# Keys' norms and factors computed between the query projections, queries' norms between the inverse levels, sums of squares taken as rows

## The reference, cut to what matters

```python
q = _short_conv(hidden_states @ Wq.T, conv_q)   # 4 taps over time, then silu; the same for k and v
beta = sigmoid(hidden_states @ Wb.T)
q = q * rsqrt(sum(q * q, -1) + 1e-06)           # per token and head; the same for k
A = where(tri_strict, -((k * beta) @ k.T), 0)   # in chunks of 32 tokens
T = solve_triangular(eye - A, eye, lower=True)
u = T @ (v * beta);  w = T @ (k * beta)
attn = where(causal, q_i @ k_i.T, 0)
o = p0 * fir3(v) + p1 * fir15(v) + p2 * fir63(v) + p3 * delta_out + p4 * v
```

## Time and profile before

| | |
|---|---|
| median of 3 runs (lowest to highest) | 488.44 us (485.57 to 488.8) |
| the profiled execution: its time / its span | 488.29 us / 486.5 us |
| busy in the span | TensorE 92%, VectorE 65%, ScalarE 34%, GpSimd 16% |
| mean granted TensorE clock | 0.969 of 2.4 GHz |

### The profile page before, as it was taken

The page is one execution under the profiler, slowest core; times in us unless marked ns, Lnnn a source line. Parts: engine busy times, 40 slices in busy tenths (PEclk is TensorE's granted clock), DMA queues, the critical chain, the costliest instruction groups (busy, mean ns, idle before and its releaser), DMA issues.

```text
span 486.5 us, 8118 instructions
## 1 busy us (share of the span) xinstructions
PE 445.5 (92%) x3154; PEld 290.7 (60%) x3154; DVE 317.7 (65%) x596; ACT 164.6 (34%) x208; POOL 78.7 (16%) x77
## 2 busy tenths in 40 slices
PE   1998889899998997899999979999998899999985
PEld 1962334335554574658776537886445688888862
DVE  5441134567993889998647874552214999999955
ACT  2001211255730010113233153204005788788730
POOL 2000000000004590001552110047200000000061
PEclk9998999999998599999978999999999999999998
DMA  8999916934040415006400020037607999999644
GB/s 323 427 427 424 428 58 248 294 76 98 1 172 14 130 49 159 3 1 259 177 3 0 2 86 0 1 120 234 231 1 292 371 398 381 384 420 385 240 113 167
DMA packets 17937, 92.41 MB, mean 190 GB/s; under 512 B 3424, under 2 KB 5104, under 8 KB 10736
## 3 DMA queue, kind: packets, MB, share of 16 engines
q1 hardware_dynamic: 14880, 78.82, 42.9%
q10 hardware_dynamic: 1488, 8.93, 5.3%
q0 software_dynamic: 1536, 4.20, 2.6%
HBM read 82.25 MB, written 12.08 MB: 194 GB/s over the span
## 4 chain that ended last, share of the span: by engine, by line
PE 75%; DVE 18%; issue 3%; ACT 2%; POOL 1%; DMA 1%; SPq 0%; DVEq 0%; ACTq 0%
PE bank L823 32%; PE bank L664 7%; PE bank L599 5%; PE bank L632 5%; PE bank L526 3%; PE bank L496 3%; PE bank L547 3%; PE bank L506 3%; DVE ring L1337 3%; DVE part L1337 3%; PE bank L648 2%; PE bank L800 1%; PE bank L649 1%; POOL small L415 1%; DVE ring L1426 1%
## 5 line engine op out<-in xcount | busy, mean ns | idle before, releaser
L599 PE MATMUL bank<-xnT,ring 128*128 128x512 f32 x96 | 43.2, 599 | 0.7 <-ACT xnT L962 0.7
L1337 DVE SCALAR_TENSOR_TENSOR part<-ring,cols,part 128x504 f32<-128x504 f32 (+13 forms) x64 | 42.6, 728 | 0.1
L664 PEld LDWEIGHTS bank<-ring 64*64 64x64 f32 x960 | 33.3, 140 | 14.2 <-issue 13.2
L664 PE MATMUL bank<-ring 64*64 64x64 f32 (+1 forms) x960 | 37.7, 231 | 2.9 <-issue 2.7
L632 PE MATMUL bank<-early,ring 128*32 128x512 f32 (+15 forms) x512 | 35.2, 422 | 1.4 <-DVE early L1360 1.4
L415 POOL TENSOR_TENSOR small<-small 128x1 f32<-128x1 f32 (+2 forms) x11 | 11.3, 1025 | 154.4 <-DVE small L1224 81.1
L1337 DVE SCALAR_TENSOR_TENSOR ring<-bank,cols,ring 128x504 f32<-128x504 f32 (+2 forms) x36 | 26.4, 734 | 12.6 <-ACT ring L1009 11.6
L599 PEld LDWEIGHTS bank<-xnT,ring 128*128 128x128 f32 x96 | 17.6, 190 | 20.9 <-issue 20.0
L632 PEld LDWEIGHTS bank<-early,ring 128*32 128x32 f32 x512 | 14.4, 114 | 18.2 <-issue 12.9
L1073 ACT ACTIVATE ring<-bank 128x256 f32<-128x256 f32 x20 | 7.7, 384 | 50.3 <-PE bank L664 49.9
L1115 ACT ACTIVATE rows<-bank 128x512 f32<-128x512 f32 x19 | 11.4, 599 | 36.0 <-PE bank L823 36.0
(11 more groups left out here) (245 smaller groups left out, 914.6 us busy)
## 6 DMA issues: line engine op xcount, KB each, us to landing
early<-wffn_in SPq DMA_DIRECT2D x21, 1024.0 KB, 8.1
ring<-ctxT_in SPq DMA_DIRECT2D x4, 2048.0 KB, 27.3
ring<-ctx_in SPq DMA_DIRECT2D x4, 2048.0 KB, 31.7
raw1b<-wffn_in SPq DMA_DIRECT2D x6, 1024.0 KB, 9.7
raw3b<-wffn_in SPq DMA_DIRECT2D x6, 1024.0 KB, 7.6
raw2b<-wffn_in SPq DMA_DIRECT2D x6, 1024.0 KB, 8.5
ring<-firw_in SPq DMA_DIRECT2D x4, 1024.0 KB, 5.2
xs<-zeros_in ACTq DMA_DIRECT2D x1, 3840.0 KB, 13.9
```

The lines of the kernel that those rows point to most:

```text
L599: last = pe.matmul(bank[5 + g % 3][:, :], wqkv[:, j, c, h * P:(h + 1) * P], xnT[:, c, :], start=(c == 0), stop=(c == DC - 1))
L664: last = pe.matmul(dst[s, d], left[s, L * t:L * (t + 1)], right(s, t), start=True, stop=True)
L1337: return dve.scalar_tensor_tensor(out=d, in0=s, scalar=w, in1=d, op0=ALU.mult, op1=ALU.add)
```

## The change

Names as before; lines move by up to 140, so the pieces name functions.

- A head's sum of squares is no longer 4 products with one output column. Squares of four heads are kept, `sum_rows` sums them as four rows of 32 partitions in a bank (4 products of 32x512 side by side), ScalarE copies the bank, and `turn_sums` turns it into 16 columns (4 products of 4 columns). It is done twice, for the keys behind projections 9 and 10, for the queries behind the keys' products. The power on GpSimd is twice 16 columns wide.
- The keys' power, table (4 rows, `ct_k`), factors, scaling and masking come before and around the last projection and its convolution; the queries' (20 rows, `ct_q`), their factors, scaling, scores and masks between the steps of the first pair of levels.
- v is transposed behind projections 8 to 11, and ScalarE scales it by beta in 4 pieces of 128 columns a head (VectorE did it whole). Tap 0 of the two short filters goes to ScalarE too (`tap0_done`).
- The long filter of head 0 begins behind projection 9, head 1's stretches into the levels, heads 2 and 3 take 4 rounds a step. The weights have three places in place of two and are loaded from projection 4 on, each as its part of the projections' weights is done with.
- Twelve 20-column gate instructions become three of 80; twelve for the table become three. Both `keep_warm` calls of the stage go. Projections use banks 1, 5, 6.

```diff
+                    sp.wait_ge(S["qkv_done"], H * (h + 1))
+                else:
+                    sp.wait_ge(S["fir_done"], 1)
+                i = h % 3
+                sp.dma_start(flat[:, FIRN * i:FIRN * (i + 1)], firw_in[h]).then_inc(ld_firw[h], 16)
 
             build_stack(0)
...
+            load_firw(2)
             build_stack(2)
-            load_firw(2)
+            load_firw(3)
             build_stack(3)
-            load_firw(3)
             sp.wait_ge(S["fir_done"], H)
-            sp.wait_ge(S["sumsq_done"], 2 * H)
+            sp.wait_ge(S["sumsq_done"], 2)
 
...
-            def sumsq(i):
-                pe.wait_ge(S["sq_done"], i + 1)
+            def sum_rows(k):
+
+                pe.wait_ge(S["sq_done"], H * (k + 1))
+                for i in range(H):
+                    last = pe.matmul(bank[4][CG * i:CG * (i + 1), :], ones[:, 0:1].broadcast_to([P, CG]), sq_b[:, i, :],
+                                     start=True, stop=True)
+                last.then_inc(S["cols_done"], 1)
+
+            def turn_sums(k):
+
+                pe.wait_ge(S["cols_kept"], 2 * k + 1)
                 for t in range(NT):
-                    last = pe.matmul(bank[4][:, 256 + NT * i + t:257 + NT * i + t], sq_b[:, i % 2, t * P:(t + 1) * P],
-                                     ones[:, 0:1], start=True, stop=True)
+                    last = pe.matmul(bank[4][:, 16 * k + t:16 * (k + 1):NT], sum_row[:, t * P:(t + 1) * P],
+                                     ident[:, 0:P:CG], start=True, stop=True)
                 last.then_inc(S["sumsq_done"], 1)
+
+            def fir_rounds(h, lo, hi):
+
...
-            for h in range(H):
-                pe.wait_ge(S["silu_done"], h + 1)
-                if h == 2:
-                    keep_warm(bank[2][:, :], 4)
+                if 2 * H - 1 <= g < 3 * H - 1:
+                    turn_v(g - 2 * H + 1)
+                if g == 2 * H:
+                    fir_rounds(0, 0, 4)
+                    sum_rows(0)
+                if g == 2 * H + 1:
+                    turn_sums(0)
+                if g == 2 * H + 2:
+                    fir_rounds(0, 4, 8)
+                    turn_table(1, 3, 20, 24)
+
...
+                    spread(bank[4 + k % 2][:, :], ct_q, (k // 4) * NPROB + (0, 1, 2, 4)[k % 4]).then_inc(S["bc_done"], 1)
 
             def between_first(step):
 
-                fir_rounds(2 + step // NLV, FW * (step % NLV) // NLV, FW * (step % NLV + 1) // NLV)
+                if step == 0:
+                    fir_rounds(1, 10, 13)
+                if step == 1:
+                    fir_rounds(1, 13, FW)
+                    turn_table(2, 4, 0, H * NPROB)
+                if 2 <= step < 6:
+                    fir_rounds(2, 4 * (step - 2), 4 * (step - 1))
+                if step >= 6:
+                    fir_rounds(3, 4 * (step - 6), 4 * (step - 5))
+                if step in (3, 4):
+                    pe.wait_ge(S["ct_lo"], 2)
+                    query_factor(2 * step - 6)
+                    query_factor(2 * step - 5)
+                if step == 6:
+                    query_scores(0)
+                    query_scores(1)
+                if step == 7:
+                    query_scores(2)
+                if step == 8:
+                    query_scores(3)
...
                 if j > 0:
-                    i = g - H
-                    act.wait_ge(S["silu_done"], g + 1)
-                    if i >= 2:
-                        act.wait_ge(S["sumsq_done"], i - 1)
-                    act.activation(sq_b[:, i % 2, :], plane[j][:, h], ACT.Square).then_inc(S["sq_done"], 1)
-
+                    act.activation(sq_b[:, h, :], plane[j][:, h], ACT.Square).then_inc(S["sq_done"], 1)
+                else:
+                    for medium, last_tap in ((0, KS - 1), (1, KS + KM - 1)):
+                        w = C_FIR + h * (KS + KM) + last_tap
+                        act.activation(branch[medium][:, h], vP[:, h], ACT.Copy,
+                                       scale=cols[:, w:w + 1]).then_inc(S["tap0_done"], 1)
+
+                act.wait_ge(S["cols_done"], 2 * k + 2)
+                act.activation(table[:, 0, :], bank[b][0:table.shape[0], :], ACT.Copy).then_inc(S["cols_kept"], 1)
+
+            def scale_values(h):
+
+                act.wait_ge(S["vt_done"], h + 1)
+                for t in range(NT):
+                    ts = slice(t * P, (t + 1) * P)
+                    ins = act.activation(bv[:, h, ts], bank[2 * (h % 2)][:, ts], ACT.Copy, scale=beta[:, t, h:h + 1])
...
             lag0(0)
             for g in range(1, 3 * H):
+                if g == 2 * H + 1:
+                    keep_sums(0)
+                if g == 3 * H - 1:
+                    keep_table(0, ct_k, 3)
                 lag0(g)
...
                     gate_exp(g - H - 1)
+                if g >= 2 * H:
...
+
+            convolve(0)
+            for g in range(1, H):
+                convolve(g)
+                fir_taps(g - 1, g)
+            convolve(H)
+            fir_taps(3, 6)
+            convolve(H + 1)
+            gating_1()
+            clear_heads(0)
+            fir_taps(6, 7)
+            convolve(H + 2)
+            gating_2()
+            convolve(H + 3)
+            clear_heads(1)
+            fir_taps(7, 8)
+            convolve(2 * H)
+            gating_3()
+            fir_taps(8, 12)
+            want_powers(0)
+            convolve(2 * H + 1)
+            key_table()
+            fir_taps(12, 13)
+            convolve(2 * H + 2)
+            fir_taps(13, 17)
+            table_low(0, ct_k, 3)
+            for h in range(H):
+                scale_key(h)
+            convolve(3 * H - 1)
+            mask_keys(0)
+            mask_keys(1)
+            want_powers(1)
+            mask_keys(2)
+            mask_keys(3)
...
+
             for n in range(2 * NLV):
-                if n in (0, NLV - 1):
-                    clear_heads(2 + (n > 0))
-                fir_taps(first + taps * n // (2 * NLV), first + taps * (n + 1) // (2 * NLV))
+                if n == 1:
+                    query_table()
+                if n in (2, 5):
+                    clear_heads(2 + n // 5)
+                if n == 3:
+                    table_low(1, ct_q, 4)
+                if n in (4, 5):
+                    scale_query(2 * n - 8)
+                    scale_query(2 * n - 7)
+                if n == 7:
+                    mask_scores(0)
+                    mask_scores(1)
+                if n == 8:
+                    mask_scores(2)
+                if n == 9:
+                    mask_scores(3)
```

269 lines of the change are left out of this document (135 added, 134 removed).

## The result

| | before | after |
|---|---|---|
| median (lowest to highest) | 488.38 us (485.08 to 489.65), 10 runs | 490.42 us (489.91 to 491.26), 10 runs |
| ratio after/before, 95% interval | | 1.0061 (1.0035 to 1.0087) |
| profiled execution: time / span | 488.29 / 486.5 us | 490.5 / 488.7 us |
| mean granted clock | 0.969 | 0.962 |
| first projection to the experts' first product | 202.0 us | 205.0 us |

The change costs about 2 us. 485.8 had been forecast, a gain of 2.5. The last row of the table is the stretch with all that the change touches, and what follows it on unchanged code. It starts with the first projection (89.69 before, 88.68 after) and ends with the first product of the shared experts (291.72 and 293.70). What is left of the span behind it is 194.8 and 195.0 us. So it is the stretch by which the kernels are compared here.

The account below looks back on a forecast made before the run. It took the stretch from 89 to 225 as bound by a row of waits and slow products. About 9 us saved at full clock less 6.5 for half clock gave 488.3 - 2.5 = 485.8 us, range 478.5 to 491.

Parts of the forecast that it names:

- TensorE up to the last projection: TensorE's work through the last projection, sums out, filter rounds and v in: end moves from 137.5 to 144.7.
- The wait that is added: Behind the last projection the first key factor waits for ScalarE's scaled v: TensorE stands 3.3 us, until 148.0.
- The clock: TensorE behind the added wait: half clock from 148 to 164.5, 6.5 us lost.
- GpSimd's power of 16 columns: The power on GpSimd, now 16 columns wide: 2.9 us, where 32 columns took 5.44.
- The levels: First pair of levels, VectorE setting the pace: 46.4 us from 168.4 to 214.8 at full clock, against 224.9 before.
- The sum: Whole kernel: about 9 us saved at full clock, 6.5 lost to half clock, so 2.5 saved.
- the slower rival: Half clock in TensorE's pauses inside the levels makes VectorE wait, about 10 us more: 495.8 us, chance 0.14.
- Its lesser form: Within the levels, only one group of products ahead of VectorE's masks runs at half clock: 490 us.
- The first rival: The clock stays full behind the last projection despite the added wait: 479.3 us, chance 0.28.
- Its signs of being wrong: ScalarE's pieces 0.6 each, added wait under 1.5, filter weights after 127, or clock dips elsewhere; expected no VectorE level wait over 3.

Follow-up runs that it names:

- e2: Changed kernel with four unread products filling TensorE's pause behind the last projection, the wait itself kept: 487.65 us, ratio 0.9957.
- e3: Changed kernel with GpSimd's ten mask products of the second pair held until 8 updates of the first: 488.88 us, ratio 0.9987.
- e4: Changed kernel with VectorE making the first update and the query table ahead of seven filter taps: 489.26 us, ratio 0.999.
- e6: Changed kernel with GpSimd's ten mask products of the second pair started after 7 updates, where VectorE waits for scores: ratio 0.9941.
- e11: Changed kernel with the edits of e1 and e7, and GpSimd's second-pair products split, two after 7 updates, eight after the first pair: 474.72 us, ratio 0.9728.
- e7: Changed kernel with TensorE making query factors and scores ahead of the four filter rounds of the same step: ratio 0.9994.
- e12: e11 plus the edit of e4 (first update and query table ahead of seven taps): 475.83 us, ratio 0.9715.
- e1: Changed kernel with ScalarE scaling the last head of v ahead of tap 0 of the last projection: 483.72 us, ratio 0.9868.

## Why the prediction was wrong, by its own steps

- **TensorE up to the last projection**: right in its end, 144.4 against 144.7, with some luck. The wait for the filter's weights is 2.2 in place of 0.5, near the upper bound of 2.6 given; the stage began 1.0 earlier, and the other terms came out 1.0 smaller.
- **The wait that is added**: right. 3.03 us against 3.3, four pieces in 1.12 against 1.2.
- **The clock**: the fall was forecast rightly, the return wasn't. Half clock from 147.6 to 157.8, not 148 to 164.5. The forecast let it return 3.5 us into head 1's round 0; that round began at 159.5, when the clock was full already. e2 puts the price at 3.2, forecast 6.5. In e3, e4 and e6, with the same pause, the half clock lasted 6.8 us and cost 1.6.
- **GpSimd's power of 16 columns**: right, 2.9.
- **The levels**: this is the step that failed. "Together 46.4 from 168.4": the three taps ahead of that point ended at 171.9, and from there to 227.6 it took 55.7. 9.3 us were missing. Counted from VectorE's rows, contention makes 5.7 of it, where the text had "about 0.6 more": four of the seven taps 1.8, four taps of the next step 1.0, the query table 2.9 (4.04 against the 1.16 of e11). Waits make 3.8: 2.3 for the factors and 4.3 for the scores, 6.6 in place of 2.8, as both stood behind filter rounds that ran partly at half clock. The two together are 9.5. e6 and e7 bear out both: they take 4.0 and 4.7 out of the levels, although e6 leaves the seven taps slow.
- **The sum**: with the clock's 6.5 the forecast has the levels from 174.9 to 221.3. They began 3.0 us earlier and lasted 9.3 longer, so they ended 6.3 late. The working gave a gain of 10.1 at full clock and the forecast took 9 of it, and the rest was 0.7 shorter: 2.5 - 6.3 + 1.1 + 0.7 is the loss of 2.0.
- **The rivals**: the slower rival had half clock inside the levels, and that came (178 to 188.5 and 205.6 to 209). The place it named and the price of 10 were wrong: the pause there is made by a slowed VectorE. Its lesser form, 490, is the number that came out, but not by that mechanism alone. The first rival, that the clock holds, fell.
- **Its signs of being wrong**: two came. The clock dipped elsewhere, and VectorE waited over 3 us in the levels (4.3 for the scores).

Both errors could be read in the trace of before. The clock: the prediction judged a pause by its length, 1.46 us harmless and 1.89 not. But before, the clock is at half from 146 to 149.5 too, and no wait of TensorE in the 6 us ahead of that was over 0.5; ahead of the half clock from 159.7 the longest was 1.4. The window:

```profile
146.00:148.00 2.00, 2.00 (x12) 0.81 (x15) 0.53 (x4) 0.00 (x0) 1.20 (x1) 0.51 0.03 8
```

The contention: this row of VectorE lies beside GpSimd's 16.51 us of mask products there:

```profile
175.65 7.78 DVE L1337 SCALAR_TENSOR_TENSOR part<-ring,cols,part 128x504 f32<-128x504 f32 x8
```

0.97 each, against 0.64 in the earlier trace rows: the price was there to be read, and the question not asked was which operations the change puts beside those products. Before, 6.0 of the 16.5 us lay beside such taps, ahead of the levels, and the scores' masks came after them; TensorE waited 1.3 us there. The change put seven taps, a table of six small instructions and four more taps there, in front of updates and a table that TensorE waits for. The plan itself was not far off: with most of the contention and of the two waits taken away (e12) the levels take 52.7 us, and the working of the prediction at full clock gives 52.9 from the power at 161.9 to 214.8. That the two are so near is in part luck, since e12 waits 0.3 us for the scores and none for the factors, where the working has 2.8, and waits elsewhere.

## What to carry to other kernels

When a change moves work on VectorE, lay GpSimd's timeline beside the new place and count every operation with both inputs in SBUF at the contended price; moving GpSimd's work to where VectorE waits or reads PSUM was worth 4 us here, with one line. An engine that holds up another's start must not do its spare work first: ScalarE's piece of 1.1 us, with what it held up, cost 6.6, of which 3.2 was the clock. A long wait of TensorE isn't its own length in time: the 7.2 us one, cut to 2.2, shortened the levels by 2.0, and on top of e1 by 1.2 and the time by nothing that can be told.

## What the runs showed that had not been expected

- A VectorE instruction of 16 columns takes 0.17 to 0.2 alone and 0.63 to 0.71 beside GpSimd's products, 3.5 times as long; a tap only 1.75 times. Short instructions suffer most.
- The slowing isn't a full turn-taking. From 168.55 to 176.30 seven taps (0.64 alone, 4.5 us) and eight products (0.69 alone, 5.5 us) fit into 7.75 us, not into 10. The Trainium skill (SBUF — State Buffer, SBUF: two separate sides) says that whichever of the two starts first has the shared ports for the whole instruction and the other is blocked; by that, an estimate from the times alone, they would need 10. The trace doesn't agree with that here, and the measurement decides.
- The same pause behind the last projection (3.0 us) brought the half clock from 147.6 to 157.8 in the changed kernel and from 149.7 to 156.5 in e3, 3.4 us less. From the start of the last projection to the power it took 24.3 us and 22.8.
